# Attention stage: who adds the weights, where Pool multiplies, how weight splits are cut, and where the last sums are made

## The reference

```python
q = x @ Wq            # 32 heads of 32, four query heads share one key/value head
k, v = x @ Wk, x @ Wv # 8 heads of 32
s = (q @ k.T) / sqrt(32), causal
p = exp(s - max) ;  ctx = (p @ v) / p.sum(-1)
```

## Time and profile before

| what | value |
|---|---|
| median of 3 runs | 2479.36 us (2478.67 to 2483.72) |
| the profiled execution | 2481.49 us |
| its span | 2479.8 us, so 1.7 us lie around it |
| the loop of stage C, first addition of head 0 to last addition of head 15 | about 1107 to 1948 us |
| busy, whole span | PE 88%, DVE 56%, POOL 40%, ACT 37% |
| granted clock, mean | 0.935 |

### The profile page before, as it was taken

One profiled execution on the slowest core, in us unless ns is written; L12 is line 12 of the kernel. 1 busy time (PEld: TensorE's weight loads), 2 busy tenths in 40 slices (PEclk: granted clock), 3 DMA queues, 4 the chain that ended last, 5 costly groups with the idle time before them and its releaser, 6 DMA issues.

```text
span 2479.8 us, 30808 instructions
## 1 busy us (share of the span) xinstructions
PE 2174.6 (88%) x11008; PEld 1540.6 (62%) x11008; DVE 1395.7 (56%) x3135; ACT 918.7 (37%) x1625; POOL 983.3 (40%) x754
## 2 busy tenths in 40 slices
PE   4899956799999968789899889898887499999998
PEld 4655534688888858655555555555543287667676
DVE  7866766677677742375555555555553155553333
ACT  4654533332323222134444454444445122221111
POOL 1334654544444410016655556466656422110000
PEclk9899977899999979889999899999987699999999
DMA  5220345121221146322224522322222354334332
GB/s 162 74 86 9 139 145 187 49 77 69 74 88 68 64 158 231 97 48 57 57 66 126 149 70 62 79 65 57 61 57 66 139 192 162 127 119 170 110 111 94
DMA packets 139568, 249.27 MB, mean 101 GB/s; under 512 B 26885, under 2 KB 69765, under 8 KB 139191
## 3 DMA queue, kind: packets, MB, share of 16 engines
q1 hardware_dynamic: 130711, 230.51, 29.3%
q10 hardware_dynamic: 8704, 16.78, 2.0%
HBM read 139.48 MB, written 76.02 MB: 87 GB/s over the span
## 4 chain that ended last, share of the span: by engine, by line
PE 59%; POOL 17%; DVE 7%; issue 6%; ACT 4%; DMA 3%; SPq 3%; POOLq 0%; DVEq 0%; ACTq 0%
POOL c_S L2180 13%; PE PS L2363 4%; PE PS L2320 4%; PE PS L2324 4%; PE PS L2321 4%; PE PS L1069 3%; PE PS L1070 3%; PE PS L1071 3%; PE PS L1831 3%; PE PS L1815 3%; PE PS L1846 2%; PE PS L1102 2%; PE PS L1104 2%; PE PS L1103 2%; PE PS L621 2%
## 5 line engine op out<-in xcount | busy, mean ns | idle before, releaser
L1980 ACT ACTIVATE c_P<-PS 128x512 f32<-128x512 f32 (+3 forms) x768 | 355.3, 493 | 387.1 <-PE PS L1831 334.7
L2180 POOL TENSOR_TENSOR c_S<-c_S,c_P 128x2048 f32<-128x2048 f32 (+1 forms) x96 | 337.0, 3510 | 12.7 <-ACT c_P L1980 6.4
L1815 PE MATMUL PS<-c_K,c_Q 96*128 96x512 f32 (+3 forms) x768 | 280.6, 376 | 54.6 <-DVE cst L2097 33.1
L1831 PE MATMUL PS<-c_Q,c_K 97*128 97x512 f32 (+3 forms) x768 | 293.3, 395 | 12.2 <-ACT c_P L1980 7.7
L1831 PEld LDWEIGHTS PS<-c_Q,c_K 97*128 97x128 f32 x768 | 153.5, 202 | 186.8 <-issue 82.6
L2093 DVE TENSOR_REDUCE cst<-PS 128x1 f32<-128x512 f32 x256 | 176.2, 688 | 137.5 <-PE PS L1815 137.1
L2163 POOL TENSOR_SCALAR_AFFINE_SELECT c_P<-c_P 128x512 f32<-128x512 f32 x128 | 85.2, 666 | 358.4 <-ACT c_P L1980 358.4
L1815 PEld LDWEIGHTS PS<-c_K,c_Q 96*128 96x128 f32 x768 | 155.9, 203 | 102.9 <-DVE cst L2097 49.2
L1846 PE MATMUL PS<-c_P,c_V 128*32 128x512 f32 (+3 forms) x1536 | 180.8, 545 | 38.1 <-POOL c_P L2163 27.2
L2097 DVE CUSTOM_DVE_ANT_0 PS<-PS,maskw 128x128 f32<-128x128 f32 (+3 forms) x256 | 126.6, 510 | 118.7 <-PE PS L1815 118.4
L199 POOL TENSOR_TENSOR maskw<-maskw,mhalf 128x1 f32<-128x1 f32 x64 | 36.6, 571 | 361.4 <-DVE maskw L168 361.4
(11 more groups left out here) (278 smaller groups left out, 4831.4 us busy)
## 6 DMA issues: line engine op xcount, KB each, us to landing
a_xin<-in_x SPq DMA_DIRECT2D x32, 512.0 KB, 4.3
c_Q<-c_qh SPq DMA_DIRECT2D x256, 64.0 KB, 2.0
d_x<-scr SPq DMA_DIRECT2D x32, 512.0 KB, 4.0
scr<-a_xin SPq DMA_DIRECT2D x16, 512.0 KB, 5.5
scr<-a_hid SPq DMA_DIRECT2D x16, 512.0 KB, 3.2
b_xn<-scr SPq DMA_DIRECT2D x16, 512.0 KB, 5.6
b_x<-scr SPq DMA_DIRECT2D x16, 512.0 KB, 4.8
scr<-b_x SPq DMA_DIRECT2D x16, 512.0 KB, 2.6
```

The costliest lines, as they stand in the source:

```text
L1815: e.matmul(bank[:, 0:hi - lo], self.Q4[0:96, 4 * (o % 3) + g, 128 * t:128 * t + 128], self.K4[0:96, HEADS[o % 8], lo:hi], start=True, stop ...
L1831: e.matmul(self.k.bank(i % 3)[:, 0:hi - lo], self.K4[0:97, HEADS[o % 8], 128 * kt:128 * kt + 128], self.Q4[0:97, 4 * (o % 3) + g, lo:hi], ...
L1980: e.activation(self.P[:, R % 3, g, 0:hi - lo], self.k.bank(i % 3)[:, 0:hi - lo], ACT.Exp, scale=SCALE).then_inc(self.exp_s.s, 1)
L2180: e.tensor_tensor(S[:, :, 512 - n:512], before[:, :, 512 - n:512], P[:, :, 0:n], ADD).then_inc(self.psum_s.s, 1)
```

## The change

- In heads 0 to 14 the first addition (rounds 4 and 5) goes from Pool to DVE, in four pieces of 512 columns, one for each g, in slots 24 to 27 behind the maximum of the slot. Pool's additions begin with round 6 and wait for the four pieces. The exponentials of rounds 7 and 8 wait for the piece of their own g.
- Pool multiplies in rounds 1 (even half of the head before) and 5 (odd half), where it multiplied in 8 and 11. The store of the even half goes from slot 52 to slot 58, counted from its head's slot 0.
- The split of a job's weights and of `wo` is cut into four pieces for ACT and for DVE, one per slot from slot 18 on (two per slot where the next job comes soon). The load of the next weights is issued three slots later, and that of `wo` seven slots ahead of its use and no longer ten.
- In head 15 neither DVE nor Pool adds anything: PE sums all rounds 4 to 11 from `c_P`, behind each product with V, and the last evacuation waits for that product.

```diff
     def adds(o, r):
-        return 7 * o + max(r, 5) - 4
+        return 6 * o + r - 5
...
-    FINISH = (8, 12, 16, 19, 36)
+    FINISH = (8, 12, 16, 19, 42), (8, 12, 16, 19, 36)
...
+                for q in range(4):
+                    self.split_at.setdefault(slots[15] + 2 + q // (2 if soon else 1), []).append((n + 1, q))
...
-                if S + 10 in WO:
-                    self.sp_wo(e, WO.index(S + 10))
+                if S + 7 in WO:
+                    self.sp_wo(e, WO.index(S + 7))
...
-        if half == 0:
+        if half == 0 or o == 15:
             m = self.pe_sums(e, o, r)
...
         self.pe_pv(e, 15, 11)
-        self.pe_sum(e, 15)
...
+    def act_w4(self, e, n, q):
+        if n < len(JOBS) + 1:
+            e.wait_ge(*self.wld[n % 2](n // 2 + 1))
+            e.wait_ge(*self.qmm_s(2 * n - 2))
+            e.copy(self.wh[:, 2 * q:2 * q + 2, :], self.raw[:, 2 * q:2 * q + 2, :]).then_inc(self.whi_s.s, 1)
...
         if g == 0 and R >= 3:
             e.wait_ge(*self.pv_s(R - 2))
-            if (R - 3) % 12 >= 4:
-                e.wait_ge(*self.psum_s(self.adds(*divmod(R - 3, 12))))
+        if R >= 3:
+            o3, r3 = divmod(R - 3, 12)
+            if r3 in (4, 5) and o3 < 15:
+                e.wait_ge(*self.pair_s(4 * o3 + g + 1))
+            elif r3 > 5 and o3 < 15 and g == 0:
+                e.wait_ge(*self.psum_s(self.adds(o3, r3)))
...
+    def dve_w4(self, e, n, q):
+        if n < len(JOBS) + 1:
+            cs = slice(2 * q, 2 * q + 2)
+            e.wait_ge(*self.whi_s(self.pieces(n - 1) + q + 1))
+            e.tensor_tensor(self.wl[:, cs, :], self.raw[:, cs, :], self.wh[:, cs, :].bitcast(F32), SUB).then_inc(self.wlo_s.s, 1)
...
+    def dve_pair(self, e, o, g):
+        e.wait_ge(*self.exp_s(48 * o + 21 + g))
+        if o > 0:
+            e.wait_ge(*self.sum_s(o))
+        a, b = (self.P[:, (12 * o + r) % 3, g, :] for r in (4, 5))
+        e.tensor_tensor(self.S[:, g, :], a, b, ADD).then_inc(self.pair_s.s, 1)
...
+                if 24 <= s < 28 and o < 15:
+                    self.dve_pair(e, o, s - 24)
...
-                if r == 8 and o > 0:
-                    self.pool_mul(e, 2 * o - 1)
-                if r == 11:
-                    self.pool_mul(e, 2 * o)
-                if r < 5:
+                if o > 0 and r in (1, 5):
+                    self.pool_mul(e, 2 * o - (2 if r == 1 else 1))
+                if r < 6 or o == 15:
                     continue
...
-                if r == 5:
-                    before = self.P[:, (12 * o + r - 1) % 3, :, :]
-                    if o > 0:
-                        e.wait_ge(*self.sum_s(o))
+                if r == 6:
+                    e.wait_ge(*self.pair_s(4 * o + 4))
                 else:
                     e.wait_ge(*self.psum_s(adds))
-                e.tensor_tensor(S[:, :, 512 - n:512], before[:, :, 512 - n:512], P[:, :, 0:n], ADD).then_inc(self.psum_s.s, 1)
+                e.tensor_tensor(S[:, :, 512 - n:512], S[:, :, 512 - n:512], P[:, :, 0:n], ADD).then_inc(self.psum_s.s, 1)
                 adds += 1
+        self.pool_mul(e, 30)
         self.pool_mul(e, 31)
```

More of the change, by code:

```diff
@@ L1503, in __init__ @@
          self.whi_s, self.wlo_s, self.amax_s, self.mx_s, self.mtr_s, self.mtc_s, self.score_s, self.exp_s, self.diag_s,
-         self.psum_s, self.pv_s, self.sum_s, self.evv_s, self.evs_s, self.rec_s, self.mul_s) = k.sigs(
-            "c_", "given xtr xhi xlo vmm vcp qmm qhi qlo whi wlo amax mx mtr mtc score exp diag psum pv sum evv evs rec mul")
+         self.pair_s, self.psum_s, self.pv_s, self.sum_s, self.evv_s, self.evs_s, self.rec_s, self.mul_s) = k.sigs(
+            "c_", "given xtr xhi xlo vmm vcp qmm qhi qlo whi wlo amax mx mtr mtc score exp diag pair psum pv sum evv evs rec mul")
         self.x0 = [k.used["x"][i] + k.extra[i] for i in range(4)]
@@ L1525, in tables @@
                 self.place_at[place[0]], self.place_at[place[1]] = (n, 0), (n, 1)
-                self.split_at[slots[15] + 2] = n + 1
+                soon = n + 1 < len(JOBS) and JOBS[n + 1][1][0] < slots[15] + 8
+                for q in range(4):
+                    self.split_at.setdefault(slots[15] + 2 + q // (2 if soon else 1), []).append((n + 1, q))
         self.bank_of, self.held_by = {}, {}
@@ L1580, in job_bank, with pieces @@
     @staticmethod
+    def pieces(n):
+        return n + 1 if n < 7 else 4 * n - 17
+    @staticmethod
     def job_bank(n, part):
@@ L1607, in sp_w @@
             if n > 1:
-                e.wait_ge(*self.wlo_s(1 if n == 2 else n))
+                e.wait_ge(*self.wlo_s(1 if n == 2 else self.pieces(n - 1)))
             e.dma_start(self.raws.get(n, self.raw[:, :, :]), self.weight(n).rearrange("(c p) n -> p c n", p=128)).then_inc(self.wld[n % 2].s, 16)
@@ L1613, in sp_wo @@
         n = len(JOBS) + 1 + c
-        e.wait_ge(*self.wlo_s(n))
+        e.wait_ge(*self.wlo_s(self.pieces(n - 1)))
         e.dma_start(self.raw[:, :, :].rearrange("p c n -> p (c n)"), self.k.io["wo"][128 * c:128 * c + 128, :]
@@ L1683, in sp_finish @@
                         ).then_inc(self.ctx[E % 2].s, 16)
-    FINISH = (8, 12, 16, 19, 36)
+    FINISH = (8, 12, 16, 19, 42), (8, 12, 16, 19, 36)
     def finish_at(self, S, step):
-        o, s = divmod(S - self.FINISH[step], 48)
-        return 2 * o - 1 if s == 0 and o > 0 else 2 * o if s == 16 and o >= 0 else None
+        first, second = ((S - f[step]) // 48 if (S - f[step]) % 48 == at else -1 for f, at in zip(self.FINISH, (16, 0)))
+        return 2 * first if first >= 0 else 2 * second - 1 if second > 0 else None
     def sp(self, e):
@@ L1725, in sp @@
                     self.sp_place(e, *self.place_at[S])
-                if S in self.split_at:
-                    self.sp_w(e, self.split_at[S] + 2)
-                if S + 10 in WO:
-                    self.sp_wo(e, WO.index(S + 10))
+                for n, q in self.split_at.get(S, ()):
+                    if q == 3:
+                        self.sp_w(e, n + 2)
+                if S + 7 in WO:
+                    self.sp_wo(e, WO.index(S + 7))
                 if s == 40 and o < 15:
@@ L1777, in pe_job @@
             if part == 0:
-                e.wait_ge(*self.wlo_s(self.piece_of(n) + 1))
+                e.wait_ge(*self.wlo_s(self.pieces(self.piece_of(n))))
             if what == 8:
@@ L1858, in pe_sums @@
         kt, lo, hi = ROUNDS[r]
-        bank = self.pe_turn(e, o, 49) if kt == 0 else self.turn_bank(o, 49)
+        half = lo // 512
+        turn = self.sum_turn(2 * o + half)
+        bank = self.pe_turn(e, *turn) if kt == 0 else self.turn_bank(*turn)
         for g in range(4):
-            m = e.matmul(bank[32 * g:32 * g + 32, lo:512], self.k.ones[:, 0:32], self.P[:, (12 * o + r) % 3, g, 0:hi - lo],
-                         start=kt == 0, stop=kt == 3, skip_group_check=True)
+            m = e.matmul(bank[32 * g:32 * g + 32, lo - 512 * half:512], self.k.ones[:, 0:32],
+                         self.P[:, (12 * o + r) % 3, g, 0:hi - lo], start=kt == 0, stop=kt == 4 * half + 3, skip_group_check=True)
         return m
@@ L1984, in act_evac @@
         if sums:
-            if E % 2:
+            if E == 31:
+                e.wait_ge(*self.pv_s(192))
+            elif E % 2:
                 e.wait_ge(*self.sum_s(E // 2 + 1))
@@ L2034, in act @@
                     self.act_job(e, *self.evac_at[S])
-                if S in self.split_at:
-                    self.act_w(e, self.split_at[S] + 1)
-                if S in WO:
-                    self.act_wo(e, WO.index(S))
+                for n, q in self.split_at.get(S, ()):
+                    self.act_w4(e, n + 1, q)
+                for q in range(4):
+                    if S - q in WO:
+                        self.act_wo(e, WO.index(S - q), q)
                 if S in RELOAD:
@@ L2139, in dve @@
                     self.dve_job(e, *self.evac_at[S])
-                if S in self.split_at:
-                    self.dve_w(e, self.split_at[S] + 1)
-                if S in WO:
-                    self.dve_wo(e, WO.index(S))
+                if 24 <= s < 28 and o < 15:
+                    self.dve_pair(e, o, s - 24)
+                for n, q in self.split_at.get(S, ()):
+                    self.dve_w4(e, n + 1, q)
+                for q in range(4):
+                    if S - q in WO:
+                        self.dve_wo(e, WO.index(S - q), q)
                 E = self.finish_at(S, 2)
```

16 lines of the change are left out of this document (8 added, 8 removed).

## The result

| | before | after |
|---|---|---|
| median of 4 runs each, same chip | 2479.15 us (2478.67 to 2483.72) | 2442.62 us (2440.39 to 2445.43) |
| ratio, with 95% interval | 1 | 0.9849 [0.9832, 0.9866] |
| profiled execution, its span | 2481.49, 2479.8 us | 2444.48, 2442.8 us |
| granted clock, mean | 0.935 | 0.946 |
| busy: PE, DVE, ACT, POOL | 88%, 56%, 37%, 40% | 89%, 60%, 38%, 36% |

A forecast was written before the change was run, and what follows sets the result against it. Pool was taken to bound 30.6 us of a head, PE, ACT and DVE by turns 21.3. Ten heads at 2.3 us, 1.6, 2 x 0.5, -1.0, 0.7 and 10 gave 35.3 us: 2444 against the median, range 2422 to 2468.

The forecast's parts named there:

- The multiplications: Ordinary heads: moved to rounds 1 and 5, where Pool is idle, they cost nothing; gain 2.5 us a head.
- The first addition: Ordinary heads: with DVE's four pieces, round 6's addition starts 5.6 us after the old start; 0.9 us a head lost.
- The quarters: Split in four from slot 18: PE's 1.59 us wait shrinks; gain 0.7 us a head, bounds 0 and 1.6.
- Heads 4 and 8: Long heads with an extra job, said to hang on SP: gain 0.5 us each from the smaller pieces.
- the part on other heads: Heads outside the ordinary ten: heads 4 and 8 gain 0.5 us each, 12 gains 1.6, 13 loses 1.0, 14 gains 0.7.
- the change leaves that queue's order: Heads 4 and 8: SP's queue of issues, on which their long part hangs, was said to keep its order.
- Heads 13 and 14: Heads with wo splits: pieces may wait for Pool's additions; net loss 1.0 us in 13, gain 0.7 in 14.
- Head 15: PE summing alone: 22.0 us from round 4's product to the last evacuation; gain 10 us, ends 6 and 14.
- The sum: Whole kernel: all terms together gain 35.3 us, giving 2446.2 us profiled, 2444 against the median.
- PE as the bound: Rival: pieces get through early and a head reaches PE's floor of 47.9 us; about 2424 us, chance 0.2.
- only the end: Rival: ordinary heads gain 0.2 us each, the end 10, heads 13 and 14 lose 3; about 2470 us, chance 0.2.
- The slower case: Rival: DVE in slots 18 to 27 becomes the bound with 1.32 us pieces; 20 us slower, about 2499, chance 0.06.

The follow-up runs named there:

- e2: Changed kernel with Pool's multiplications back in rounds 8 and 11 and the even half's store back in slot 52: 2457.58 us, ratio 0.9904.
- e1: Changed kernel with the first addition (rounds 4 and 5) back on Pool, in round 5 behind the odd half's multiplication: 2458.70 us, ratio 0.9905.
- e3: Changed kernel with every weight split whole again (one cast, one subtraction) and wo's load at its old distance: 2452.53 us, ratio 0.9882.
- e9: e5 with the eight wo splits moved to slots where Pool adds nothing, loads five slots ahead: 2435.69 us, ratio 0.9829.
- e7: Changed kernel with the odd half's multiplication moved from round 5 to just behind round 6's addition: 2444.57 us, ratio 0.9847.
- e4: Kernel before the change with only head 15's rounds 4 to 11 summed on PE: 2470.25 us, ratio 0.9955.
- e5: Changed kernel with whole splits where the next job comes soon, mask row loaded ahead of wo, even half's store in slot 61: 2437.21 us, ratio 0.9814.
- e8: e5 with rounds 9, 10 and 11 summed on PE in heads 0 to 14: 2429.79 us, ratio 0.9806.
- e6: e5 with rounds 10 and 11 summed on PE in heads 0 to 14: 2436.04 us, ratio 0.9819.
- e0: The changed kernel run once more, unaltered, beside e8 and e9: 2441.31 us, ratio 0.9847.

## Why the prediction was right, and where it was not

**The multiplications.** Forecast 2.5 us off Pool's chain, measured 2.2 (e2 against the changed kernel). In head 11 the broadcast is there in time, as told: Pool's wait before the multiplication of round 5 ends with ACT's exponentials. What the forecast booked under the next step, the first piece stuck behind the multiplication, makes the net 1.35 (e2).

**The first addition.** Forecast: round 6 at 5.6 us, 0.9 later than before. Measured 5.2, 0.5 later; e1 shows that it would be 5.9 with the addition left on Pool. The reading was right in kind: the four pieces take 0.68 us, the first waits 0.89 (forecast 0.9), and the addition moved to another engine gains 0.7 a head and no more. Of the two prices in the earlier trace rows the lower one held, as Pool is idle. The higher one, 1.32, was a misreading: it is the mean of two kinds. Of its 32 subtractions 19 ran with no Pool instruction beside them and took 0.68 or 0.69 us, and 13 ran beside one and took 1.11 to 2.48. One of each kind, in stage D:

```profile
2029.99 2.48 DVE L2435 TENSOR_TENSOR d_xl<-d_in,d_xh 128x512 fp32r<-128x512 f32 x1 [1.82 <-ACT d_xh L2392]
...
2037.43 0.68 DVE L2435 TENSOR_TENSOR d_xl<-d_in,d_xh 128x512 fp32r<-128x512 f32 x1
```

So the trace did have the price of a piece alone. The chain up to the end of the last addition was 23.7 us for a forecast of 23.4.

**The quarters.** This is the term that was mis-sized: 0.7 forecast, 1.2 in the timeline (20.1 us for 21.3) and 2.0 by e3. The 1.59 us of the earlier trace rows went, and only small waits took its place (0.16 us there, 0.33 and 0.34 behind the pieces of the addition); I had charged the additional instructions with most of it. PE's waits in an ordinary head fell from 5.0 to 2.9 us. A head thus won 3.1 us instead of 2.3 in eight of the ten periods, and all ten won 29.1 instead of 23.

**Heads 4 and 8.** Forecast a gain of 0.5 each. Measured a loss of 9.1 in head 4 and 0.6 in head 8. The step that failed is in the part on other heads: I wrote "Pool isn't late there" and then looked for the lock of the earlier trace rows only at `wo`. A split by quarters reaches over more slots, in head 4 into slots 34 and 35, where Pool adds, and two pieces of 0.4 us each stood for one addition of 4.5. The same rule that I used for head 13 was due for every split that can come beside an addition. e3 gives the split 6.3 of the 9.1 us. The second slip was "the change leaves that queue's order": the store moved to slot 58 now comes between the weights' load and the sums' load in head 5, or ahead of both. That this costs anything isn't shown. Most of the other 2.8 us goes with a slower landing of the sums (7.47 us in e3 for 5.17), but the landing took 7.96 us in e2 with the old order, and its cause stays open.

**Heads 13 and 14.** Forecast a loss of 1.0 in head 13; measured a gain of 2.6, though the mechanism is there. DVE's timeline in head 13:

```profile
1805.15 4.67 DVE L2095 TENSOR_TENSOR c_xtl<-c_raw,c_xth 128x256 fp32r<-128x256 f32 x1 [1.72 <-ACT c_xth L1948]
...
1811.11 3.05 DVE L2095 TENSOR_TENSOR c_xtl<-c_raw,c_xth 128x256 fp32r<-128x256 f32 x1
```

Two pieces are stuck, 4.67 and 3.05 us for one of 0.45, as the prediction said, and PE pays about what it said: behind them it waits 1.74 and 0.91 us for maxima, 2.65 for a forecast of 3. What it overlooked is that the old period was no clean one. These are Pool and PE of the kernel before, from slot 40 of head 13 on:

```profile
1828.39 5.49 POOL L2180 TENSOR_TENSOR c_S<-c_S,c_P 128x2048 f32<-128x2048 f32 x1
...
1834.61 1.51 PE L1846 MATMUL PS<-c_P,c_V 128*32 128x384 f32 x8 [3.73 <-POOL c_P L2163]
```

There the whole subtraction (from 1828.06 on) had already made an addition 5.49 us long, and PE stood 3.73 us for a mask that Pool made late; its longest wait in the period is now 2.17. PE's waits of over 0.4 us add up to 9.8 us in the old period and 6.5 in the new one. So Pool's relief was worth more here than the 2.5 booked, because PE had been waiting for it. In head 14 the forecast was a gain of 0.7 and the measure is -0.1 (from round 6 to head 15's product of round 4, 45.9 us for 45.8). The chain shows what I left out:

```profile
1858.32 8.77 DVE c_xtl L2095 x3
...
1867.56 3.48 DMA c_Q<-c_mT
...
1871.08 1.22 PE PS L1840 x2
```

Three pieces wait 8.77 us. SP's next `wo` load waits for them, and the mask row for head 15 (`c_mT` into `c_Q`) stands behind it in the queue, so PE's scores wait too. The prediction had counted that no maxima stand behind these pieces, and not what stands behind them on SP. Whole splits would have done better here (41.8 us in e3), and so do quarters where Pool adds nothing (42.2 in e9): the quarters cost 4.1 us in this head.

The Trainium skill (SBUF — State Buffer, section "Who interferes with whom") calls the ports that VectorE and GpSimd share an exclusive lock, and says, of VectorE's two-port modes, that whoever issues first has them for the whole instruction. e7 agrees for this addition from two SBUF tiles (1631 to 693 ns), and the piece of head 4 took 4.76 us beside an addition of 4.50. The price that matters is therefore the length of Pool's instruction, and for a shorter piece of DVE it is a larger share.

**Head 15.** Forecast 22.0 us from round 4's product to the evacuation, measured 22.4 (1892.65 to 1915.05). The clock in that window is 0.92 (before 0.66), as the prices for the two levels assumed. Gain 10.5 with the rest as before; forecast 10 with the wait for `wo`, of which ACT had 0.5.

**The sum.** The forecast of 35.3 us against 37.0 is better than its terms, by luck. The misses were +6.1 in the ordinary heads, -10.7 in heads 4 and 8, +3.6 in head 13, -0.8 in head 14, +1.0 in head 12 and behind head 14, and +2.5 outside these stretches: 13.2 us one way and 11.5 the other.

**The rivals.** PE as the bound (2424) didn't come about: the period ended 1.1 us above its floor of 47.9 and PE had 2.9 us idle. It is nearer than "only the end", since e4 shows that the end alone gives a quarter. The slower case fell with the 0.68 us of the pieces. That the forecast's total may hide large terms of opposite sign was not among my cases; taking 8.2 of the 9.1 us lost in head 4 out gives 2437 us (e5).

## What to carry to other kernels

Before an operation is cut into pieces, look at each place where a piece can now run beside the engine that shares its ports: a piece pays the whole instruction of the other engine, and what stands behind it on its own engine and on the DMA queue pays too. Check a schedule change in the irregular passes as well as in the pattern pass, for the regular ones here gained 29 us and one irregular one lost 9. Don't take one trace for the price of a transfer: the same load, issued in the same order, landed after 5.17 us in one kernel and 7.96 in another. When a chain that bounded a loop has been shortened, stop shortening it once the period no longer follows (23.7, 18.7 and 14.6 us gave 49.0, 49.2 and 49.4) and spend the effort where time is still lost.

## What the hardware showed that was not expected

- A small subtraction of 128 x 256 from SBUF takes 0.41 to 0.58 us alone and took 4.67, 3.05 and, as a row of three, 8.77 us beside Pool's additions. In the row two were held up, 4.42 and 3.64 us. The lock works both ways: an addition of Pool took 5.33 and 5.49 us instead of 4.56 behind a whole subtraction.
- Fewer matmuls in a stretch need not make it shorter. In head 13, with no job's steps between the scores, PE ran 233 instructions in 48.3 busy us at a granted clock of 0.72 (e9) and in 44.3 at 0.79 (e5), where 283 took 46.1 at 1.00 in an ordinary head. In e8, where PE sums three rounds more, 259 took 43.0 at 0.90, and the period was 1.8 us shorter than in e5.
- The small load of sums in head 5 took 5.17 to 7.96 us in twelve traces, and what SP issues just ahead of it doesn't sort them: with the weights' load alone ahead 5.17, 6.17, 7.96, 5.56, 7.29, 5.83 and 7.73 (before, e4, e2, e5, e6, e8, e9), with the store as well 7.17, 7.01, 6.27, 7.47 and 7.00 (changed, e0, e1, e3, e7).
